# Attention over a context in 56 tiles per layer: all score products of the next tile ahead of the twelve turned blocks

## What is computed

```python
qh = (q_in @ wq + bq).reshape(b, q_len, H, K)
kh = (kv_in @ wk + bk).reshape(b, t, H, K)
vh = (kv_in @ wv + bv).reshape(b, t, H, K)
kh = jnp.concatenate([kh, jnp.broadcast_to(bias_k, (b, 1, H, K))], axis=1)
vh = jnp.concatenate([vh, jnp.broadcast_to(bias_v, (b, 1, H, K))], axis=1)
logits = jnp.einsum('bqhk,bthk->bhqt', qh, kh) / scale
weights = jax.nn.softmax(logits, axis=-1)
ctx = jnp.einsum('bhqt,bthk->bqhk', weights, vh).reshape(b, q_len, H * K)
return ctx @ wo + bo
```

## Time and profile before

| | us |
|---|---|
| median of 3 runs | 1966.26 |
| lowest, highest | 1960.67, 1976.54 |
| the profiled execution, its own time | 1976.77 |
| its span, first to last instruction | 1975.0 |
| PE busy in it | 1739.3 |
| DVE busy | 1257.6 |
| ACT busy | 1023.0 |
| POOL busy | 482.0 |

### The profile page before, as it was taken

The page is one execution under the profiler, slowest core; times in us unless marked ns, Lnnn a source line. Parts: engine busy times, 40 slices in busy tenths (PEclk is TensorE's granted clock), DMA queues, the critical chain, the costliest instruction groups (busy, mean ns, idle before and its releaser), DMA issues.

```text
span 1975.0 us, 32767 instructions
## 1 busy us (share of the span) xinstructions
PE 1739.3 (88%) x9974; PEld 1486.3 (75%) x9974; DVE 1257.6 (64%) x2513; ACT 1023.0 (52%) x1857; POOL 482.0 (24%) x334
## 2 busy tenths in 40 slices
PE   2388888888759999999999998699999999999986
PEld 2377777777647888888888886578888888888875
DVE  3376666676567666666656657776666666666574
ACT  2265666575435555555555546355555455555462
POOL 4264454552134011011101103440110011011042
PEclk7799999999779999999999998899999999999988
DMA  6645667654224011001001102240110011010021
GB/s 188 157 125 148 163 164 179 154 137 119 63 64 145 9 60 62 31 31 62 32 31 62 62 1 67 77 138 19 45 62 31 31 62 48 15 62 0 1 67 52
DMA packets 113905, 149.50 MB, mean 76 GB/s; under 512 B 25433, under 2 KB 99681, under 8 KB 113833
## 3 DMA queue, kind: packets, MB, share of 16 engines
q1 hardware_dynamic: 113832, 148.61, 27.2%
HBM read 108.28 MB, written 3.42 MB: 57 GB/s over the span
## 4 chain that ended last, share of the span: by engine, by line
PE 63%; issue 7%; DVE 4%; POOL 2%; ACT 2%; DVEq 0%; PEld 0%; POOLq 0%; PEldq 0%; ACTq 0%
PE ps L893 16%; PE ps L662 10%; PE ps L664 10%; PE ps L663 10%; PE ps L895 8%; PE ps L863 7%; PE ps L874 1%; POOL cx L631 1%; PE ps L762 0%; DVE rr L1540 0%; POOL khl L503 0%; DVE o_row L1562 0%; ACT o_low L1232 0%; PE ps L968 0%; POOL raw_t L514 0%
## 5 line engine op out<-in xcount | busy, mean ns | idle before, releaser
L893 PE MATMUL ps<-cx,rr 128*128 128x512 f32 x1344 | 484.6, 403 | 15.8 <-DVE rr L1540 14.0
L1216 ACT ACTIVATE rr<-ps 128x512 fp32r<-128x512 f32 x336 | 198.7, 597 | 349.7 <-PE ps L863 349.7
L895 PE MATMUL ps<-cx,rr 128*128 128x256 f32 x1344 | 374.8, 279 | 0.0
L893 PEld LDWEIGHTS ps<-cx,rr 128*128 128x128 f32 x1344 | 252.4, 188 | 74.6 <-issue 19.4
L662 PE MATMUL ps<-ct,rr 128*128 128x500 f32 x672 | 280.7, 418 | 6.6 <-ACT ar L1200 6.6
L1540 DVE TENSOR_TENSOR rr<-ps,rr 128x512 fp32r<-128x512 f32 x336 | 231.4, 690 | 55.5 <-ACT rr L1216 40.0
L664 PE MATMUL ps<-ct,rr 128*128 128x500 f32 x672 | 261.7, 389 | 0.0
L663 PE MATMUL ps<-ct,rr 128*128 128x500 f32 x672 | 260.7, 388 | 0.0
L895 PEld LDWEIGHTS ps<-cx,rr 128*128 128x128 f32 x1344 | 253.9, 189 | 0.0
L1562 DVE SCALAR_TENSOR_TENSOR o_row<-ps,rinv,o_low 128x256 f32<-128x256 f32 x112 | 54.1, 483 | 309.9 <-ACT o_low L1232 309.9
L1514 DVE TENSOR_REDUCE mx<-ps 128x1 f32<-128x500 f32 x336 | 226.8, 676 | 11.7 <-PE ps L664 3.5
(11 more groups left out here) (183 smaller groups left out, 3221.8 us busy)
## 6 DMA issues: line engine op xcount, KB each, us to landing
raw_t<-in_ctx_t SPq DMA_DIRECT2D x24, 1500.0 KB, 6.4
k<-khl SPq DMA_DIRECT2D x192, 187.5 KB
raw<-in_ctx SPq DMA_DIRECT2D x24, 1408.0 KB
raw<-stat_scratch SPq DMA_DIRECT2D x8, 750.0 KB, 4.0
ar<-in_wq SPq DMA_DIRECT2D x32, 128.0 KB, 3.5
ar<-in_wk SPq DMA_DIRECT2D x32, 128.0 KB, 3.6
ar<-in_wv SPq DMA_DIRECT2D x32, 128.0 KB, 2.2
ar<-in_wo SPq DMA_DIRECT2D x32, 128.0 KB, 2.1
```

The lines of the kernel that those rows point to most:

```text
L893: pe.matmul(ps[:, 6, :], pt[0:n, 0, c, :], cx[0:n, c, :], start=c == 0, stop=False, skip_group_check=True)
L895: mm = pe.matmul(ps[:, 6, 0:D], pt[0:n, 1, c, :], cx[0:n, c, 0:D], start=False, stop=c == CH - 1, skip_group_check=True)
L1216: act.activation(pt[:, 0, GRP * k:GRP * (k + 1), :], ps[:, 3 + k, :].rearrange("p (c q) -> p c q", q=P), ACT.Copy)\
```

## The change

In `batch` of PE's list, the three thirds of the next tile's scores come first, and then the three groups of turned blocks; before they alternated. In `batch` of DVE's list, the three maxima and the negated one come first, and then the three low parts; before they alternated as well. ACT's, POOL's and SP's lists stay as they are. No instruction is added or removed, no tensor moves, and the values computed are the same.

```diff
@@ PE, batch
                     for k in range(3):
                         if not (last and t == TILES - 1):
                             scores(r, nb, nt, g + 1, k)
+                    for k in range(3):
                         transposes(r, g, k)
                     turn_output(r, g - 1)
                     weighted(r, b, t, g)
@@ DVE, batch
                     end = last and t == TILES - 1
+                    if not end:
+                        for k in range(3):
+                            row_max(r, g + 1, k)
+                        neg_max(r, g + 1)
                     for k in range(3):
-                        if not end:
-                            row_max(r, g + 1, k)
-                        if k == 2 and not end:
-                            neg_max(r, g + 1)
                         low_probs(r, g, k)
```

## The result

The changed kernel takes 2084.66 us in the median of 4 runs (2079.79 to 2090.42), the kernel before 1971.4 us (4 runs, 1960.67 to 1981.52, with those known at the time of the prediction). The ratio is 1.0576, 95% interval 1.0507 to 1.0646: 113 us slower. The profiled execution took 2087.51 us, 110.7 more than that of before.

A forecast was written before the change was run, and what follows sets the result against it. The prediction took PE to bound the kernel, working nearly without a break. Its terms, 67 + 22 + 17 + 24 = 130 us, took the median from 1966.26 to 2096 us, with a range of 2080 to 2115.

The forecast's parts named there:

- PE's own work: PE's turned blocks and scores in 110 rounds: taken as 0, between 0 and a gain of 20 us.
- The wait ahead of the weighting, ordinary rounds: PE waits for DVE's low part until T + 2.10 to 2.34 (T: first turned block's start): 96 x 0.70 = 67 us.
- The first round of a batch: Round t = 0: maxima ahead of DVE's low part lengthen PE's wait by 1.57 us, 14 x 1.57 = 22 us.
- The round t = 5: ACT's late splits of `ct` delay POOL, DVE and PE's next scores by 1.1 to 1.4 us: 17 us.
- PE's clock: Half clock for 3.4 us behind each longer wait in round t = 0: 14 x 1.7 = 24 us.
- The sum: All terms over the kernel: 67 + 22 + 17 + 24 = 130 us slower, median 2096 us.
- The idle time in the profile: Sign in the groups: 95 to 120 us idle ahead of the weighting in place of 15.8, released by DVE's low part.
- The rival of a full clock: The waits come at changes of batch too, but PE's clock stays full: 106 us slower, 2072 us; chance 0.20.
- That DVE catches up at the changes of batch: Rival: changes of batch add nothing, only the ordinary wait counts: 67 us slower, 2033 us; chance 0.13.
- That PE's order would gain time: Rival: two fewer returns from turned blocks to scores on PE save 20 us, 1946 us; chance 0.02.
- The copy that might have waited for POOL: DVE's copy (line 1518) in round t = 0: might wait 0.5 us for POOL, 7 us in all; counted as nothing.

The follow-up runs named there:

- The run with the blocks first: Kernel before, with all twelve turned blocks ahead of the next tile's scores and DVE's low parts ahead of its maxima: 1981.51 us, ratio 1.0041.
- The run with both moves: Changed kernel, with ACT's splits of `ct` ahead of its high parts (t = 5) and DVE's split of `cx` late in t = 0: 2040.22 us.
- The run with ACT's splits ahead: Changed kernel, but in round t = 5 ACT splits thirds 0 and 1 of the next context ahead of its high parts: 2069.51 us, ratio 1.0448.
- the run with one group early: Kernel before, with one group of turned blocks ahead of the scores' last third, two behind, DVE's order following: 1990.24 us, ratio 1.0070.

## Why the prediction was right

The forecast was 130 us slower, 2096 against 1966; measured are 113 us. The main mechanism and each of its places stand; the sizes by its own terms:

- *PE's own work:* forecast 0. The run with the blocks first has the same twelve in a row, and its ordinary round is as long as before, 9.77 us; its 7 us are a longer wait for the exponential. The gain of up to 20 us that I left open didn't come.
- *The wait ahead of the weighting, ordinary rounds:* forecast T + 2.10 to T + 2.34 and 0.70 us; the trace has T + 2.10 and 0.65 us, 96 x 0.65 = 62 us. The round takes 10.42 or 10.51 us, as forecast. The run with both moves, 65 us slower, shows this term nearly by itself.
- *The first round of a batch:* forecast 1.57 us more; the idle time went from 1.05 to 2.53, 1.48 more, 14 x 1.48 = 21 us. The run with PE's order alone gave it back, so DVE's order is the cause of this term and PE's order of the first. (My 14.0 us of waits before weren't one at each change of batch: 12 of them were, two were the last tiles of the layers with 0.90 each, and the other two changes, 0.88 and 0.89, are printed as waits for ACT. The sum is 14 us all the same.)
- *The round t = 5:* forecast a wait of 1.1 to 1.4 us by way of ACT, POOL and DVE; the scores start 5.38 us behind the weighting's start, where 4.32 was, 1.06 more. From this weighting to the next there are 11.66 us, where there were 9.82, of which 0.66 are the next round's ordinary wait: 14 x 1.18 = 16 us. The run with ACT's splits ahead removed it, 24 us less in the tiles; some 6 of these are that its trace has 7 half-clock stretches in place of 11.
- *PE's clock:* this is the term that was mis-sized. I counted half clock behind all 14 waits, 24 us. It came behind 11, and each cost 1.6 us by the rounds' lengths (12.00 against 10.44), 17 us together. What decides between the 11 and the 3 the runs don't show; the waits are alike (2.3 to 2.6 us). That waits of 0.7 and 1.2 us are without effect held.
- *The sum:* 62 + 21 + 16 + 17 = 116 us, against 116.3 in the tiles, 110.7 between the whole profiled executions and 113 between the medians.
- *The idle time in the profile:* forecast 95 to 120 us ahead of the weighting, printed are 76.7. This sign missed. I had set 0.70 us for each ordinary wait, but the profile prints only 0.41 of its 0.65, because it counts the matmul before it as busy beyond the moment at which the next one could have started: 96 x 0.24 = 23 us of the wait stand in no group. The waits are there, the page counts them as busy.

The rival of a full clock (106 us) is excluded by the rows at 0.50, and not by its time: as a difference it lies nearer to the 113 us measured than the forecast's 130 does. That 2096 is 11 us from 2084.66 and the rival's 2072 is 13 is luck of the base, 1966.26 then and 1971.4 with one run more. That DVE catches up at the changes of batch falls by the timeline at 780.27. That PE's order would gain time fell with the wait itself: the low part would have had to be done by T + 1.31, and was at T + 1.96.

The copy that might have waited for POOL ran at 778.91 in 0.14 us, inside POOL's operations (773.67 to 779.43). The Trainium skill (SBUF — State Buffer, Who interferes with whom) says that DVE's copies can contend with GpSimd when their operands meet certain conditions; this copy of one element per partition didn't wait. The same section of the Trainium skill says that a DVE instruction with two SBUF inputs contends with a GpSimd one that reads SBUF, and the traces agree: 2.34 us for a product of 128x1 beside POOL's split, and 0.22 with a scalar operand.

## What to carry to other kernels

A block of PE work that another engine must post-process belongs as far ahead of its use as the post-processing takes: here 2.1 us from the first block to the first use, which 1.45 us of PE work didn't cover and a third of the scores more did. Follow, for every step that is moved, the first output that the next consumer needs, not the sum of the work, and do it again at each irregular round: nearly half of this loss (54 of 116 us) lay in the 28 rounds around changes of batch. A wait can cost more than its length: a wait of 1.9 us was followed by the half clock in 6 of 12 cases, at 1.5 us each. And where two engines hold each other up, look at the moment at which one comes: here the same split of 1.21 us took 2.27 or 2.91 us and left POOL or PE waiting, depending on whether it stood behind the first maximum or behind the first low part.

## What was not expected of the hardware

- DVE and POOL took turns at their splits. A DVE split that came at 757.01, while POOL's first of two back-to-back splits ran, got in between them and took 2.27 us; one that came at 768.51, some 0.6 us into the second, took 2.91 us and started its work only behind it. By the ratios, the whole kernel was 12 us faster with the first and 22 us slower with the second, of which some 9 us were half clock. In both cases the work itself seems to be the usual 1.21 us at the end; this is worked out from the lengths and not seen in the trace.
- Waits of 2 us were enough to be followed by 3.4 us of half clock, in some cases and not in others. Behind waits of 2.3 to 2.6 us the clock fell in 11 of 14 cases in the changed kernel, and in 7 of 14 both with DVE's order alone and with the early splits of `ct`; behind those of 1.8 to 1.9 us in 6 of 12. It never fell in the tiles behind shorter ones, such as the 14 of 1.5 to 1.6 us in the run with one group early, or the 96 of 1.07 us with DVE's order alone.
- A low part started 0.07 us behind the start of a maximum of 0.16 us on the same engine (747.87, 747.94): DVE's instructions overlap at their ends, here by 0.09 us, and printed lengths don't simply add.
